# Graph attention passes: the front of a half runs two halves ahead, and the score products stand first in a half

## What is computed

```
def gat_layer(feat, src, dst, W, a, gamma, beta):
    msg = feat @ W
    attn_src = msg @ a[:dh]
    attn_dst = msg @ a[dh:]
    scores = jax.nn.leaky_relu(attn_src[src] + attn_dst[dst], ALPHA)
    scores = scores - scores.max()
    e = jnp.exp(scores)
    denom = jax.ops.segment_sum(e, dst, num_segments=n) + 1e-10
    coef = e / denom[dst]
    out = jax.ops.segment_sum(msg[src] * coef[:, None], dst, num_segments=n)
    ...  # batch norm over the nodes
```

## Time and profile before

| | |
|---|---|
| median of 3 runs | 9471.22 us (9467.75 to 9473.85) |
| profiled execution | 9472.38 us, its span 9470.8 us |
| PE / DVE / POOL busy in the span | 61% / 51% / 53% |
| pass 0 | about 283 to 3450 us |
| pass 1 | about 3470 to 6240 us |
| SAGE passes | from about 6500 us |

### The profile page before, as it was taken

The page is one execution under the profiler, slowest core; times in us unless marked ns, Lnnn a source line. Parts: engine busy times, 40 slices in busy tenths (PEclk is TensorE's granted clock), DMA queues, the critical chain, the costliest instruction groups (busy, mean ns, idle before and its releaser), DMA issues.

```text
span 9470.8 us, 196466 instructions
## 1 busy us (share of the span) xinstructions
PE 5802.7 (61%) x50950; PEld 4110.0 (43%) x50951; DVE 4811.3 (51%) x14633; ACT 3083.3 (33%) x7540; POOL 5048.4 (53%) x4726
## 2 busy tenths in 40 slices
PE   3355565555556454555555555547588877488887
PEld 2344444444444224555455555535344444244444
DVE  5344444444444645555555555555555555355555
ACT  0111111010111113444444444441255555355555
POOL 1454555546464015555555555512466666466676
PEclk9756665665666575555555555555699998799999
DMA  3222121222212442222222222202344444344444
GB/s 92 43 44 59 44 58 46 45 59 45 59 44 57 137 110 42 41 41 41 41 41 41 41 41 41 41 15 73 79 111 112 110 110 108 92 107 109 108 108 101
DMA packets 622304, 647.34 MB, mean 68 GB/s; under 512 B 343902, under 2 KB 515637, under 8 KB 621872
## 3 DMA queue, kind: packets, MB, share of 16 engines
q0 software_dynamic: 193600, 384.69, 19.3%
q1 hardware_dynamic: 356987, 238.04, 8.8%
q10 hardware_dynamic: 71640, 23.81, 1.0%
HBM read 562.39 MB, written 83.23 MB: 68 GB/s over the span
## 4 chain that ended last, share of the span: by engine, by line
issue 21%; DVE 21%; another core or an unknown queue 19%; PE 18%; DVEq 9%; DMA 5%; ACT 4%; SPq 1%; ACTq 1%; POOL 0%; POOLq 0%
PE psa L1412 7%; PE psc L1429 5%; ACT acc L1161 2%; DVE acc L1825 2%; DMA acc<-y_d 2%; DVEq L1786 1%; DVEq L593 1%; DVE den L1822 1%; DMA t_gat<-acc 1%; DVE rows L1894 1%; PE psc L1400 1%; DVEq L1790 1%; DMA t_part<-den 1%; DVE acc L1685 1%
## 5 line engine op out<-in xcount | busy, mean ns | idle before, releaser
L613 POOL DMA_INDIRECT rows<-t_gat,idx x3168 | 3081.7, 973 | 2408.9 <-issue 824.2
L633 POOL DMA_INDIRECT acc<-t_part,acc x1400 | 1795.9, 1283 | 822.1 <-issue 618.8
L1338 PE MATMUL psa<-rhs,rows 128*128 128x176 f32 (+1 forms) x6336 | 1721.4, 431 | 55.5 <-issue 33.4
L1161 ACT ACTIVATE acc<-psa 128x384 bf16<-128x384 f32 x3200 | 1345.8, 503 | 1226.2 <-PE psa L1412 656.3
L1338 PEld LDWEIGHTS psa<-rhs,rows 128*128 128x128 f32 x6336 | 1503.9, 312 | 162.8 <-issue 98.1
L1412 PE MATMUL psa<-den,rhs 125*32 125x384 bf16 x12800 | 909.0, 361 | 452.8 <-ACT acc L1161 313.4
L1326 PE MATMUL psc<-oh,wgt 128*8 128x22 f32 (+1 forms) x6336 | 294.6, 207 | 1036.3 <-ACT wgt L1067 872.1
L1061 ACT ACTIVATE oht<-psc 22x1024 bf16<-22x1024 bf16 x402 | 407.3, 1013 | 1594.1 <-remote 1110.9
L1412 PEld LDWEIGHTS psa<-den,rhs 125*32 125x32 bf16 x12800 | 296.0, 98 | 1056.1 <-ACT acc L1161 633.3
L1326 PEld LDWEIGHTS psc<-oh,wgt 128*8 128x8 f32 (+1 forms) x6336 | 238.1, 95 | 1146.4 <-ACT wgt L1067 960.6
L1067 ACT ACTIVATE wgt<-s_d 128x64 f32<-128x64 f32 (+1 forms) x396 | 93.8, 237 | 1965.4 <-DVE s_d L1742 1249.9
(11 more groups left out here) (342 smaller groups left out, 8216.4 us busy)
## 6 DMA issues: line engine op xcount, KB each, us to landing
rows<-list_src SPq DMA_DIRECT2D x200, 500.0 KB
rows<-t_gat,idx POOLq DMA_INDIRECT x3168
acc<-y_d SPq DMA_DIRECT2D x50, 1000.0 KB, 5.4
y_d<-stg SPq DMA_DIRECT2D x100, 250.0 KB, 2.0
acc<-t_part,acc POOLq DMA_INDIRECT x1400
acc<-t_sage SPq DMA_DIRECT2D x300, 62.5 KB
adw<-win_d SPq DMA_DIRECT2D x820, 2.2 KB
adw<-win_d SPq DMA_DIRECT2D x788, 0.4 KB
```

The lines of the kernel that those rows point to most:

```text
L613: eng.indirect_dma_start(rows[:, j, 0:spec["width"]], None, spec["table"], bass.IndirectOffsetOnAxis(ap=idx[:, j:j + 1], axis=0)).then_inc ...
L633: eng.indirect_dma_start(h_prow[u][:, t, :], None, t_parts[layer], bass.IndirectOffsetOnAxis(ap=h_idx[u][:, t:t + 1], axis=0)).then_inc(h_ ...
L1161: eng.activation(h_rows[:, g, :], psa[:, g % 4, 0:D3], ACT.Copy).then_inc(hyb["ev"], 1)
L1338: last = eng.matmul(sums(half, q, h), rows[:, slot * TH + j, 0:D], right, start=(j == 2 * q), stop=(j == 2 * q + 1))
```

## The change

It does four things, in the attention passes only:

1. `halves` takes a number `lead`, 2 here. DVE, PE and ACT run the front of half *m+2* inside the main part of *m*. Two fronts instead of one stand ahead of each range's loop, so that one more front runs per range. `oh` gets four buffers; `ohb` keeps two and `oht` one.
2. PE takes the scores of *m+1* at the head of half *m*, as soon as `exp_arg` of *m* is posted, ahead of its wait for the exponentials. The sums of the four pairs follow one another.
3. SP's lead stays one half, but in pass 1 the `adw` loads stand ahead of the load of the list's edges.
4. DVE no longer waits for `adx_ready` before the first one-hots of a range.

```diff
-        def halves(eng, spec, lo, hi, nxt, front, main):
+        def halves(eng, spec, lead, lo, hi, nxt, front, main):
             slots = spec["slots"]
-            front(lo, 0, True)
+            for slot in range(lead):
+                front(lo, slot, slot == 0)
             with eng.Fori(lo, hi, spec["step"]) as b:
-                for slot in range(slots - 1):
-                    main(b, slot, lambda: front(b, slot + 1, False))
+                for slot in range(slots - lead):
+                    main(b, slot, lambda: front(b, slot + lead, False))
                 ahead = next_trip(eng, spec, nxt, b)
-                main(b, slots - 1, lambda: front(ahead, 0, False))
+                for slot in range(slots - lead, slots):
+                    main(b, slot, lambda: front(ahead, slot + lead - slots, False))
...
-        oh = sb("oh", [EP, 2, TH, WIN])
+        oh = sb("oh", [EP, RING, TH, WIN])
...
+            eng.sem_inc(oht_sb, 1)
...
+                    next_front()
                     if lists and slot % 2 == 0:
                         list_load(block_of(spec, b, slot))
-                    next_front()
...
             def scores(half):
-                f = value(eng, nf)
-                eng.wait_ge(oht_sb, f)
+                eng.wait_ge(oht_sb, value(eng, nf) + 1)
...
                 if spec["weighted"]:
+                    eng.wait_ge(exp_arg, m)
+                    eng.sem_inc(alone, 1)
+                    scores(1 - half)
                     eng.wait_ge(wgt_ready, m)
...
                 next_front()
                 for q in range(PAIRS):
-                    if q == PAIRS // 2 and spec["weighted"]:
-                        scores(1 - half)
...
-                    if first and weighted:
-                        eng.wait_ge(adx_ready, f + 1)
...
-                        eng.wait_ge(adx_ready, value(eng, nf) + 2)
+                        eng.wait_ge(adx_ready, eng.snap(nk, min_val=0, max_val=MAX_HALVES) + 3)
...
-                halves(eng, spec, lo, hi, nxt, front, main)
+                halves(eng, spec, spec["lead"], lo, hi, nxt, front, main)
```

More of the change, by code:

```diff
@@ L528, in value @@
             return eng.snap(reg, min_val=1, max_val=most)
[L530 to L533, removed]
+        G0 = dict(name="g0", lead=2, slots=RING, unit=1, step=RING, table=t_gat0, width=ROW0, heads=H, weighted=True, parts=True, window=win0_d, k=K0, cols=SN, count=True, dens=H)
+        G1 = dict(name="g1", lead=2, slots=RING, unit=RING, step=1, table=t_gat1, width=ROW1, heads=1, weighted=True, parts=False, window=win1_d, k=K1, cols=N, count=True, dens=2, lists=True)
+        S0 = dict(name="s0", lead=1, slots=2, unit=2, step=1, table=t_sage0, width=D, heads=1, weighted=False, parts=False, cols=N, count=False, rest=True)
+        S1 = dict(name="s1", lead=1, slots=2, unit=2, step=1, table=t_sage1, width=D, heads=1, weighted=False, parts=False, cols=N, count=False, rest=True)
         def acc_view(spec):
@@ L818, in run @@
                 first_of_next(v, lo, w0)
-                halves(eng, spec, lo, hi, nxt[0], front, main)
+                halves(eng, spec, 1, lo, hi, nxt[0], front, main)
             def after(s):
@@ L1058, in front @@
                     eng.wait_ge(oh_ready, f)
-                    eng.activation(ohb[:, half, :, :], oh[:, half, :, :], ACT.Copy).then_inc(ohb_ready, 1)
+                    eng.activation(ohb[:, half, :, :], oh[:, slot, :, :], ACT.Copy).then_inc(ohb_ready, 1)
                 eng.wait_ge(oht_ps, f)
@@ L1082, in after @@
                     eng.activation(stg[:, u, :], psa[:, u, 0:CH], ACT.Copy).then_inc(fl_sb, 1)
-            node_ranges(eng, spec, lambda s0, v, lo, hi, w0: halves(eng, spec, lo, hi, nxt, front, main), after)
+            node_ranges(eng, spec, lambda s0, v, lo, hi, w0: halves(eng, spec, spec["lead"], lo, hi, nxt, front, main), after)
             if lists:
@@ L1294, in front @@
                     return
+                if first:
+                    eng.wait_ge(oht_sb, value(eng, nf))
+                    eng.sem_inc(alone, 1)
                 eng.wait_ge(ohb_ready, value(eng, nf))
@@ L1326, in main @@
                         last = eng.matmul(p_dens[half][0:hd, (j // 2) * WIN:(j // 2 + 1) * WIN], wgt[:, half, j, 0:hd],
-                                          oh[:, half, j, :], start=(j % 2 == 0), stop=(j % 2 == 1))
+                                          oh[:, slot, j, :], start=(j % 2 == 0), stop=(j % 2 == 1))
                     last.then_inc(den_ps, 1)
@@ L1336, in main @@
                     for j in (2 * q, 2 * q + 1):
-                        right = rhs[:, half, j, 0:h * WIN] if spec["weighted"] else oh[:, half, j, :]
+                        right = rhs[:, half, j, 0:h * WIN] if spec["weighted"] else oh[:, slot, j, :]
                         last = eng.matmul(sums(half, q, h), rows[:, slot * TH + j, 0:D], right,
@@ L1704, in front @@
                     if lists:
-                        eng.tensor_tensor(oh[:, half, :, :], iota_w[:, :].unsqueeze(1).to_broadcast([EP, TH, WIN]),
+                        eng.tensor_tensor(oh[:, slot, :, :], iota_w[:, :].unsqueeze(1).to_broadcast([EP, TH, WIN]),
                                           rel_all[:, ds(tile_at(spec, b, slot), TH)].unsqueeze(2).to_broadcast([EP, TH, WIN]),
@@ L1759, in weighted_onehots @@
                         eng.tensor_tensor(rhs[:, half, two, 0:h * WIN].rearrange("p t (h j) -> p t h j", h=h),
-                                          oh[:, half, two, :].unsqueeze(2).to_broadcast([EP, 2, h, WIN]),
+                                          oh[:, slot, two, :].unsqueeze(2).to_broadcast([EP, 2, h, WIN]),
                                           wgt[:, half, two, 0:h].unsqueeze(3).to_broadcast([EP, 2, h, WIN]),
```

4 lines of the change are left out of this document (2 added, 2 removed).

## The result

| | us |
|---|---|
| before, median of 4 runs | 9472.53 (9467.75 to 9476.55) |
| changed, median of 4 runs | 9864.22 (9856.14 to 9866.41) |
| ratio | 1.0412, 95% interval 1.0394 to 1.0430 |

A forecast was written before the change was run, and what follows sets the result against it. POOL was taken as the nearest thing to a bound, its stops for PE's sums costing the time. 9471 - 160 (pass 0) + 15 (extra fronts) - 88 (pass 1) = 9238, rounded to 9240 us, range 8800 to 9600.

The forecast's parts named there:

- I count 9.8 + 2.1 = 11.9 us for a half: Pass 0: eight gathers plus one POOL stop per half, against 12.7 us before; -160 us over 200 halves.
- part 3: Pass 1, DVE's list work: two halves take 26.3 us, the middle of 24.3 and 28.4, against 27.2; -88 us.
- Part 1: Pass 0, scores at the head: one POOL stop per half in place of 1.4; -160 us, bounds -570 to +250.
- Part 2: Fronts two ahead: six more fronts, 408 copies instead of 402; +15 us, 0 to 24.
- the upper end: Pass 1: an eight-gather run holds the `rest_counts` post throughout, so two halves take 28.4 us.
- Part 4: SP's order in pass 1, windows ahead of the list's load: cost and gain nothing.
- nothing is held: No held posts: PE's posts are not seen only 1.2 to 1.7 us behind the end of POOL's gather run.
- No held posts any more: Rival: POOL never stops in pass 0, -570 us; pass 1 falls to 24.3, -284; about 8630 us; chance 0.12.
- POOL's own floor: POOL's gathers alone: the eight of a half take 9.8 us, at 1.23 us each.
- Slower: Rival: pass 1's eight-gather runs hold `rest_counts`; 29.7 us per two halves, +245; 9571 or 9731 us; chance 0.22.
- L1654 waiting 3 us or more: Sign of the slower rival: the wait for `rest_counts` in pass 1, 1.13 us before, grows to at least 3.

The follow-up runs named there:

- g2: The change in pass 0 alone, without a break, pass 1 as in the kernel before; 9463.51 us, 1.0142 against 9334.70 before.
- e1: The change in pass 0 alone, pass 1 with lead 1 and the old order; 9465.94 us, 1.0149 against 9326.41 before.
- e3: The kernel before, lead 1, with the scores of m+1 moved behind all four pairs, so the sums go in one piece; 9878.85 us, 1.0587.
- e12: The changed kernel with SP's old order in pass 1, the list's edges ahead of the windows; 8156.39 us, 1.0107 against 8071.07 before.
- f1: The changed kernel itself, word for word, run again in the fourth group; 8145.67 us, 1.0114 against 8051.97 before.
- e2: The change in pass 1 alone, with its order on SP, pass 0 the old one; 9555.50 us, 1.0241 against 9326.41 before.
- e5: The changed kernel with POOL waiting ahead of a half's fifth gather until its first four have landed, both passes; 9516.59 us, 1.0044 against 9478.95 before.
- g1: The change in pass 0 alone, with POOL's wait ahead of the fifth gather there; 9254.47 us, 0.9915 against 9334.70 before.
- e7: The changed kernel with gathers of 32 and 172 bytes a row in place of 544 and 516, as many gathers; 9860.75 us, 1.0403 to the kernel before.
- e8: The changed kernel with 8 score matmuls in place of 24, the two correcting terms left out; 9579.19 us, 1.0109 to the kernel before.

## Why the prediction was wrong

**The step that failed** is "I count 9.8 + 2.1 = 11.9 us for a half". The count of stops was right: one per half in pass 0, runs of eight. Their length was not: 3.3 us on average in 1200 to 1500 us, which makes 13.3 us for a half. (The 9.8 is a little low too: in the timelines eight gathers of 0.94 us and 0.30 between two take 9.9 to 10.0.) I had read from three timelines that PE's *posts* are late behind a run and taken PE's *work* to go on inside it. In the changed kernel the issue of matmuls itself stalls in a run (84.2 us at L1334 and L1303 in 1200 to 1500 us). In the run of the earlier trace rows PE had issued its 40 matmuls by 1213.9 and had nothing more to show it. With longer runs, and with the scores, the denominators and the transposes in one piece inside them, the transposes and the first sums fall behind the end of the run, and POOL waits for them. In pass 1, which holds most of the loss, the same step stands in part 3 as "PE's transposes of *m+2* still end about 3.2 us behind `pen`": they end 5.2 to 8.5 us behind it, and with them `ranks` and the sums come late.

**Part 1** (-160 forecast): +106, and +129 to +139 us of the whole time where the change is in pass 0 alone (g2, e1). The pairs in one go, without the rest of the change, cost pass 0 109 us (e3). **Part 2** (+15): the six more fronts are there (408 copies); their price wasn't measured by itself. A lead of two with the scores left between the pairs was not run, so what the lead does alone is open. **Part 3** (-88 forecast, between 24.3 and 28.4 us per two halves): +289, 30.1 us. The wait of `rest_counts` on which I built the upper end did not grow but nearly went: 7.6 us in all against 49.8. In its place the denominators crawl (L1334 <- issue 160.6 us), L1638 waits 218.4 / 40 = 5.5 us per two halves against 4.07, and L1711 has stalls of up to 4.1 us, where L1705 of before has 0.4 at most. **Part 4** (nothing): no run speaks against it. In 4000 to 5200 us of the changed kernel PE's scores never wait for `adw`, and e12 and f1 are equal where nothing is held.

**The rivals.** "No held posts any more" is wrong for this change; the runs where nothing was held come near POOL's own floor, which I put at 9.8 us a half: 10.5, with the ends of the ranges. "Slower" was the right side, 9571 to 9731 against 9864, and one of its signs came, stops of POOL of 5.2 to 6.0 us once per two halves (4400 to 5000 us). The other, L1654 waiting 3 us or more, did not: its mechanism is shown in e3, not in the changed kernel. It was too low for two reasons: pass 0, which I left at -160 or nothing, loses too, and the crawl inside a run was not in it.

**What is shown and what is not.** Shown: each pass loses by itself (e1, e2); the sums in one go, with the scores behind them, are enough for a loss (e3); a pause of POOL takes most of it away (e5) and turns pass 0 into a gain (g1); the bytes don't matter (e7), the number of PE's matmuls does in the changed kernel (e8); where no post is held, the change costs 1.1% and not 4.1 (f1). Not shown: what holds PE's work while POOL gathers, why it does not happen in some groups, and whether e8's gain would appear in the kernel before too, since both its runs fell where nothing is held. Loading of instructions doesn't look like it: the profile lists 77 packets of it in a whole execution, in the changed kernel and in f1 alike. Fewer gathers, or fewer rows in one, were not tried. That late posts and slow issue are one thing is a guess that no run tests.

## What to carry to other kernels

Count not only how often the bound engine stops but what the others have to get through until it can go on, and read it from a stretch where that work lies inside the run, not behind it. Fewer, longer bursts on one engine were no gain here where they took away the gaps in which another caught up (e3, 1.0587); the pause where credit was left brought the change in pass 0 alone from 1.0142 (g2) to 0.9915 (g1). And have the kernel before beside each variant: the same kernel took 8052 us in one group and 9479 in another, and the sign of a fix depended on which.

## What was unexpected of the hardware

- PE crawled while POOL issued indirect gathers: in the changed kernel 16 denominators took 4.8 us inside a run (4525.05 to 4529.83), and 0.74 in a run of f1. DVE too had stalls without a wait that the profile shows (L1711 <- issue, up to 4.1 us; in f1 its longest wait in 4000 to 5200 us is 0.4).
- It wasn't the bytes: rows of 32 and 172 bytes in place of 544 and 516 left 1.0403 against 1.0412.
- The changed kernel had no such stalls in another group of runs: 8145.67 us (f1) against 9864.22. The kernel before took 8052 to 8071 us in two groups against 9326 to 9479 in the others, 13 to 15% less. Chip number 7 is on record with both, 9326 and 8071.
